# Signed search keys, a shorter tie step, halved first picks and a retuned order in a post-LN attention and routed-FFN kernel

## The reference

```python
qkv = x @ w_attn + b_attn
q, k, v = jnp.split(qkv, 3, axis=-1)
attn = softmax(q @ k.T / sqrt(C) + causal_mask)
x = _layernorm(x + (attn @ v) @ w_proj + b_proj)

scores = jnp.einsum('bld,d->bl', x, w_router)
_, top_idx = jax.lax.top_k(scores, k)            # k = int(0.75 * 4096)
out = x.at[batch_idx, top_idx].set(gelu(selected @ w_block))
x = _layernorm(x + out)
```

## Time and profile before

| | |
|---|---|
| three runs | 966.97, 969.17, 973.5 us |
| median | 969.17 us |
| the profiled execution's own time | 968.08 us |
| its span, from first to last instruction | 966.4 us |
| around the span | 1.68 us |
| mean granted TensorE clock | 0.989 |
| busy: PE, DVE, ACT, POOL | 939.0, 769.3, 635.3, 273.4 us |
| DMA | 149.53 MB, mean 155 GB/s |

### The profile page before, as it was taken

One profiled execution on the slowest core, in us unless ns is written; L12 is line 12 of the kernel. 1 busy time (PEld: TensorE's weight loads), 2 busy tenths in 40 slices (PEclk: granted clock), 3 DMA queues, 4 the chain that ended last, 5 costly groups with the idle time before them and its releaser, 6 DMA issues.

```text
span 966.4 us, 15640 instructions
## 1 busy us (share of the span) xinstructions
PE 939.0 (97%) x5078; PEld 805.6 (83%) x5078; DVE 769.3 (80%) x1473; ACT 635.3 (66%) x993; POOL 273.4 (28%) x436
## 2 busy tenths in 40 slices
PE   9999999999999999999999999999999999998991
PEld 7889988888888888888888999888888888887770
DVE  5688996967966786689769999887898778569977
ACT  3566675764864585478555875686688558447985
POOL 3523124253052034512214243323204302211162
PEclk9999999999999999999999999999999999999996
DMA  6535343344253345567433533535778534437935
GB/s 191 175 122 167 115 143 120 120 131 139 80 164 99 102 150 163 157 224 223 155 113 93 194 114 105 164 97 179 243 234 243 178 103 130 120 100 232 314 119 174
DMA packets 89378, 149.53 MB, mean 155 GB/s; under 512 B 7761, under 2 KB 25810, under 8 KB 89298
## 3 DMA queue, kind: packets, MB, share of 16 engines
q1 hardware_dynamic: 89298, 148.54, 48.9%
HBM read 108.66 MB, written 39.85 MB: 154 GB/s over the span
## 4 chain that ended last, share of the span: by engine, by line
PE 94%; DVE 3%; issue 1%; ACT 1%; POOL 0%; ACTq 0%; DVEq 0%; POOLq 0%
PE sbank L515 37%; PE fbank L515 13%; PE obank L1049 11%; PE obank L1051 11%; PE obank L1050 11%; PE obank L1043 2%; PE obank L1045 2%; PE obank L1044 2%; PE fbank L1340 1%; PE fbank L1139 1%; PE mbank L947 1%; PE mbank L970 1%; DVE cmp L1503 1%; PE obank L555 1%; ACT parts L996 0%
## 5 line engine op out<-in xcount | busy, mean ns | idle before, releaser
L515 PE MATMUL sbank<-qT,xT 128*128 128x512 f32 (+2 forms) x1728 | 413.2, 379 | 0.0
L515 PEld LDWEIGHTS sbank<-qT,xT 128*128 128x128 f32 x1728 | 306.4, 189 | 53.0 <-issue 0.3
L872 ACT COPY ring<-sbank 128x512 f32<-128x512 f32 (+3 forms) x288 | 157.6, 549 | 178.2 <-PE sbank L515 126.9
L1001 DVE TENSOR_TENSOR ring_lo<-ring,parts 128x1024 fp32r<-128x1024 f32 (+4 forms) x176 | 179.6, 1027 | 30.9 <-ACT parts L996 30.2
L1049 PE MATMUL obank<-ring_lo,vs 128*128 128x512 f32 x480 | 183.6, 383 | 4.3 <-ACT parts L996 2.6
L1051 PE MATMUL obank<-parts,vs 128*128 128x512 f32 x480 | 181.9, 379 | 0.0
L1050 PE MATMUL obank<-parts,vs 128*128 128x512 f32 x480 | 181.6, 378 | 0.0
L996 ACT CAST parts<-ring 128x1024 fp32r<-128x1024 f32 (+4 forms) x176 | 145.9, 834 | 51.7 <-PE obank L1051 38.9
L982 DVE TENSOR_TENSOR ring<-ring,mbank 128x1024 f32<-128x1024 f32 (+4 forms) x176 | 159.4, 946 | 9.4 <-PE mbank L970 9.4
L989 ACT ACTIVATE ring<-ring 128x1024 f32<-128x1024 f32 (+4 forms) x176 | 143.9, 844 | 24.7 <-DVE ring L982 24.4
L914 DVE TENSOR_TENSOR runmax<-ring,runmax 128x1024 f32<-128x1024 f32 x84 | 107.2, 1276 | 64.7 <-ACT ring L872 64.1
(11 more groups left out here) (222 smaller groups left out, 1203.6 us busy)
## 6 DMA issues: line engine op xcount, KB each, us to landing
vs<-v_scratch SPq DMA_DIRECT2D x288, 256.0 KB, 2.8
v_scratch<-vnew SPq DMA_DIRECT2D x30, 512.0 KB, 3.2
xres<-x SPq DMA_DIRECT2D x16, 512.0 KB, 4.6
out<-tail SPq DMA_DIRECT2D x32, 256.0 KB, 3.2
x_scratch<-xres SPq DMA_DIRECT2D x14, 512.0 KB, 3.0
y_scratch<-yb SPq DMA_DIRECT2D x14, 512.0 KB, 4.6
tail<-x_scratch SPq DMA_DIRECT2D x28, 256.0 KB, 3.5
tail<-y_scratch SPq DMA_DIRECT2D x28, 256.0 KB, 4.3
```

The costliest lines, as they stand in the source:

```text
L515: mm = eng.matmul(o, lhs(lh, k), rhs(rh, k), start=n == 0, stop=n == len(todo) - 1)
L872: act.copy(slot(n)[:, c0:], sbank[n % NSS][:, c0:]).then_inc(a_copy, 1)
L1001: dve.tensor_tensor(slots_lo(ns, c0), slots(ns, c0), f32(hi_of(u)), ALU.subtract).then_inc(v_lo, 1)
```

## The change

1. The planner's tables. `project xhi` goes from 4 to 15 and loses its margin of 2, `project vhi` and `softmax exp` lose their entries (100 and -4), `search first` goes from 60 to -4, `final pick` from 30 to -15, `ffn gelu` from 4 to 8. No other entry changes.
2. Keys. `make_keys` has three linked operations instead of four: the key stays a signed integer, its upper half is cut out with a mask instead of a shift and a multiplication, and the search of the upper half begins at -32768 * UPPER.
3. Ties. `split_ties` gets two operations more, which make one number per row out of the two marks; `select` has three linked operations instead of four.
4. The late block in the last search. `late_turn` lets each `stats` and the `aggr` of groups 14 and 15 wait for a certain comparison, for `split_ties` or for `select`; `pe_f` of the last group waits for `p_last`, a count that PE's rounds raise.
5. The first unit is picked and stored by single tiles (128 rows, 128 KB): 17 picks and 17 stores instead of 16.

```diff
-PREFER_US = {"ffn flo": 100, "final load": 100, "project vhi": 100, "ffn store": 100, "last chain": 60,
+PREFER_US = {"ffn flo": 100, "final load": 100, "ffn store": 100, "last chain": 60, "last router": 60,
...
-MARGIN_US = {"attention_out router": 3, "final scale": 3, "project xhi": 2, "ffn flo": 2, "final_roots": 2,
+MARGIN_US = {"attention_out router": 3, "final scale": 3, "ffn flo": 2, "final_roots": 2, "prepare bias": 1.5,
...
             def pe_f(pe, j, tiles_=(0, 1)):
+                if G == len(groups) - 1:
+
+                    pe.wait_ge(p_last, 2 + 2 * j + tiles_[0])
...
+            def late_turn(dve, t):
+
+                n = (G - LATE) * (QT + 1) + t
+                if n < 2 * ROUNDS - 1:
+                    dve.wait_ge(v_cmp, 2 * ROUNDS + 2 * (n + 2))
+                elif n == 2 * ROUNDS - 1:
+                    dve.wait_ge(v_sel, 2 * B)
+                else:
+                    dve.wait_ge(v_tie, B)
...
-                link(dve, dve.tensor_scalar(signs, bits, 31, -2147483648, ALU.arith_shift_right, ALU.bitwise_or))
+                signs = (mbank[:, 128:128 + NT].bitcast(I32) if b else top_keys[b])[:, k]
+                link(dve, dve.tensor_scalar(signs, bits, 31, 2147483647, ALU.arith_shift_right, ALU.bitwise_and))
                 link(dve, dve.tensor_tensor(keyi[:, 1, k], bits, signs, ALU.bitwise_xor))
-                link(dve, dve.tensor_scalar(keyi[:, 0, k].bitcast(U32), keyi[:, 1, k].bitcast(U32), 16, None,
-                                            ALU.logical_shift_right))
-                link(dve, dve.tensor_scalar(top_keys[b][:, k], keyi[:, 0, k], UPPER, None, ALU.mult))
+                link(dve, dve.tensor_scalar(top_keys[b][:, k], keyi[:, 1, k], -65536, None, ALU.bitwise_and))
...
+                dve.wait_ge(v_sel, 2 * (b + 1))
+                link(dve, dve.scalar_tensor_tensor(out=keyf[:, 2], in0=gteq[:, 0], scalar=2 * UPPER / (UPPER + TOPK),
+                                                   in1=gteq[:, 1], op0=ALU.mult, op1=ALU.add))
+                link(dve, dve.tensor_scalar(keyf[:, 2], keyf[:, 2], UPPER + TOPK, -UPPER, ALU.mult, ALU.add))
...
-                link(dve, dve.tensor_tensor_scan(ahead, ones[:, 0:2 * NT], tot, 0.0, ALU.mult, ALU.add))
-                dve.tensor_tensor(keyf[:, 2], ahead[:, NT - 1:2 * NT - 1], within, ALU.add).then_inc(v_tie, 1)
+                link(dve, dve.tensor_tensor(keyf[:, 2], keyf[:, 2], within, ALU.subtract))
+                dve.tensor_tensor_scan(ahead, ones[:, 0:2 * NT], tot, 0.0, ALU.mult, ALU.add).then_inc(v_tie, 1)
                 dve.wait_ge(v_tie, b + 1)
-                link(dve, dve.scalar_tensor_tensor(out=keyf[:, 0], in0=keyf[:, 2], scalar=float(TOPK), in1=gteq[:, 1],
-                                                   op0=ALU.is_lt, op1=ALU.mult))
-                link(dve, dve.scalar_tensor_tensor(out=left_out if b else sel[:, 1], in0=keyf[:, 0], scalar=0.0,
-                                                   in1=gteq[:, 0], op0=ALU.add, op1=ALU.is_equal))
+                link(dve, dve.tensor_tensor(left_out if b else sel[:, 1], ahead[:, NT - 1:2 * NT - 1], keyf[:, 2],
+                                            ALU.is_ge))
...
-            at("dve", "final pick", pick)
-            final_store(b, u, y, v_pick, u + 1)
+            if u:
+                at("dve", "final pick", lambda dve: pick(dve, 0, 2))
+                final_store(b, u, y, v_pick, u + 2)
+            else:
+
+                for t in range(2):
+                    at("dve", "final pick", lambda dve, t=t: pick(dve, t, t + 1))
+                    at("sp", "final store", lambda sp, t=t: store_half(sp, t))
```

More of the change, by code:

```diff
@@ L66 @@
-MARGIN_US = {"attention_out router": 3, "final scale": 3, "project xhi": 2, "ffn flo": 2, "final_roots": 2,
-             "prepare bias": 1.5, "out": 1.5, "ffn store": 1.5, "scores hide": 1, "values load": 0.6,
-             "ffn aggr": 0.6, "row_max reduce": 0.6, "values": 0.6, "project load": 0.3, "proj": 0.3,
-             "attention_out stats": 0.3}
+PREFER_US = {"ffn flo": 100, "final load": 100, "ffn store": 100, "last chain": 60, "last router": 60,
+             "project qhi": 60, "attention_out residual": 60, "project qlo": 60, "attention_out stats": 60,
+             "ffn fhi": 60, "attention_out score": 60, "row_max": 60, "final store": 60, "scores copy": 30,
+             "softmax hi": 30, "final pick": -15, "search": 30, "ffn stats": 15, "values load": 15,
+             "project xhi": 15, "prepare xlo": 8, "attention_out norm": 8, "ffn gelu": 8, "row_max reduce": 4,
+             "project vlo": 4, "softmax lo": 4, "project load": 4, "attention_out evac": 4, "prepare bias": 4,
+             "search first": -4, "scores hide": -4, "softmax z": -4, "final result": -4, "ffn add": -4,
+             "ffn aggr": -8, "attention_out router": -8, "attention_out aggr": -8, "attention_out istd": -8,
+             "last": -8, "final scale": -15, "final own": -15, "final choose": -30, "prepare": -30}
@@ L71 @@
+MARGIN_US = {"attention_out router": 3, "final scale": 3, "ffn flo": 2, "final_roots": 2, "prepare bias": 1.5,
+             "out": 1.5, "ffn store": 1.5, "scores hide": 1, "values load": 0.6, "ffn aggr": 0.6,
+             "row_max reduce": 0.6, "values": 0.6, "project load": 0.3, "proj": 0.3, "attention_out stats": 0.3}
 COSTS = {"pe": (.0, 1 / 2400, .2), "act": (.13, 1 / 1200, .14), "dve": (.09, 1 / 960, .12),
@@ L1404, in add @@
                 pool.tensor_tensor(y_pair(G, j), x1_pair(G, j), y_pair(G, j), ALU.add).then_inc(g_y, 1)
+            def late_turn(dve, t):
[6 more added lines that the diff above has]
+                    dve.wait_ge(v_tie, B)
             def stats(dve, t):
                 dve.wait_ge(g_y, 2 * G + t // 2 + 1)
+                if late:
+                    late_turn(dve, t)
                 if G and t == 0:
@@ L1412, in aggr @@
             def aggr(dve):
+                if late:
+                    late_turn(dve, QT)
                 for t in range(QT):
@@ L1438, in ffn @@
                 at("sp", "ffn store", store)
[L1441 removed]
+        SEARCH_STEPS = [3 + 2 + 2 * ROUNDS + 5, 2 * 3 + 2 + 2 * ROUNDS + 4]
         PIECES = [[(0, NT)], [(0, NT // 2), (NT // 2, NT)]]
@@ L1746, in both_outcomes, with pick @@
                 at("act", "final sums", lambda act, t=t: sums(act, t))
-            def pick(dve):
+            def pick(dve, t0, t1):
                 dve.wait_ge(v_srch, sum(SEARCH_STEPS[:b + 1]))
@@ L1815, in _ @@
             for n in range(2):
-                sp.wait_ge(st_o[n], 16 * B * NUT // 2)
+                sp.wait_ge(st_o[n], 16 * (B * NUT // 2 + (n == 0)))
         @block.gpsimd
```

14 lines of the change are left out of this document (8 added, 6 removed).

## The result

The changed kernel took 974.27 us in the median of 18 runs, the kernel before 969.14 in 18 runs beside it: a ratio of 1.005 with a 95% interval from 1.0038 to 1.0062. It is 5 us slower; the forecast was 970.5 and its range ended at 973.5. The sign was right and the size was not. The profiled execution of the changed kernel took 973.43 us, its span is 971.7 us against 966.4, so 5.3 us are to be found in the two traces. One run of all that follow, of the kernel fill_gap, took 1584.04 us where its nine others took 971 to 977, counts as slow and is left out of its ratio.

A forecast was written before the change was run, and what follows sets the result against it. PE, busy 939.0 of 966.4 us, was taken as the bound. Start +1.4, body 0 and tail -0.1 summed to +1.3, a span of 967.7, forecast as a 970.5 us median with range 967.0 to 973.5.

The forecast's parts named there:

- The pair on ACT: Start: the cast of the next group's x precedes the first queries' second half on ACT, making DVE's `qlo` 3.7 us late.
- The values begin at 21.9 instead of 20.47: +1.4 us: Start: PE waits for WV before the first values, a loss of 1.4 us; bounds +0.5 to +2.9.
- PE's own 20.9: Start, low bound: with no DVE operation slowed, the scores' end at 20.9 decides when values begin, +0.5 us.
- my bound of +2.9: Start, upper bound: both WB operations slowed and the scores' idle delaying the clock, +2.9 us.
- the tail's -0.1: Tail in all, from earlier mask and first store less store-queue gaps: about -0.1 us, bounds -0.9 to +0.5.
- The body (nothing): Body between start and tail: order swaps are covered by slack, 0 us, bounds -0.4 to +1.5; a failed cover costs 0.8 to 1.6.
- my rival of the early body: Early body: swapped casts of x wait for a load ahead of ACT's score copies, stopping PE; 972.2 us, chance 0.12.
- The search and the ties: Tail: last reduction 0.55 us earlier with the late product out of round 2's count; tie step gains 0.15.
- Picks and stores: Tail end: two statistics cost 0.66 before the first pick; half store leaves 0.32 earlier, store gaps take back about 0.28.
- The clock: Rival: pauses at the start make PE's clock rise 2.6 us later, costing 1.3 us; 971.8 us, chance 0.13.
- Not slower: Rival: x lands early or WV's slack covers the start, and the tail's gain comes through; 968.5 us, chance 0.2.
- the change doesn't do what it says: Rival: search rounds 3 and 4 lengthen by what round 2 gains, and statistics delay the picks; 971.0 us, chance 0.1.

The follow-up runs named there:

- fill_gap: Changed kernel with nine empty matmuls in PE's pause ahead of the first scores: 973.41 us, ratio 1.004 to the kernel before.
- swap_in: Kernel before with one swap on ACT: cast of the next group's x ahead of the second half of the first queries; 973.24 us, ratio 1.003.
- swap_back: Changed kernel with one swap on ACT: second half of the first queries again ahead of the cast of the next group's x; 971.1 us, ratio 1.0008.
- before_again: Kernel before, unchanged, profiled a second time: span 965.1 us.
- code_only: Changed kernel with the old planner tables, so only keys, ties, late block and halved first pick are new: 973.43 us, ratio 1.0026.
- xhi_back: Changed kernel with only the `project xhi` table entry as before (preference 4, margin 2): 969.15 us, ratio 0.999.
- after_again: Changed kernel, unchanged, profiled a second time: span 972.0 us.
- tables_only: Kernel before with the new planner tables (PREFER_US and MARGIN_US) alone: 974.4 us, ratio 1.0037.
- xres_later: Changed kernel with SP's two residual loads held back until the x of groups 1 and 2 has landed: 973.81 us, ratio 1.0027.
- best: Changed kernel, three moves: second queries before x's cast; copy near 406 before the activation; statistics and aggregation behind the fifth unit's pick. 969.08 us, ratio 1.0002.
- best_whole: Kernel best with the first unit picked and stored whole: 969.14 us, ratio 1.0002.
- best_hold: Kernel best with POOL's two subtractions for group 1 held back until both parts of WV are made: 968.59 us, ratio 1.0004.

## Why the prediction was right and wrong

**The pair on ACT.** Right, as worked out: ACT in order behind the cast, DVE in order behind `qlo`, WB's subtraction slowed to 1.65 to 1.67, its cast not (0.42), WV alone. By the Trainium skill's rule of the shared interfaces ("GPSIMD Engine Reference", section "8. Key points"), with the loser blocked ("SBUF — State Buffer", section "Terms"), I had named 22.2 for the case that both of WB's operations are blocked; the traces show the subtraction slowed and the cast not, and so the earlier value. WV's cast in the earlier trace rows had been slowed (1.55); why WB's was not stays open. I had WV ready at 21.7 to 22.2; in the five other profiles with this pair the values begin at 21.56 to 22.35. swap_in and swap_back show that the pair is the cause.

**The size of that term.** This is the step that failed: "The values begin at 21.9 instead of 20.47: +1.4 us". The first transposes of mcol, behind the start, show its whole price. Over five profiles with the old pair (before, before_again, swap_back, code_only, xhi_back) they stand at 36.11, 33.77, 36.02, 36.44 and 33.74, mean 35.2; with the new pair (after, after_again, swap_in, tables_only, xres_later) at 39.75, 39.01, 38.89, 39.57 and 39.10, mean 39.3. So the term is 4.1 us. That agrees with the 4.1 between the changed kernel and swap_back; swap_in put it at 2.9 (1.3 to 4.6). best, best_whole and best_hold have the old pair too and stand at 34.74, 37.86 and 35.00; with them the term is 3.8.

The 2.6 that I missed (4.05 less 1.43) have three parts, each rounded.

- 0.9: the base. 20.47 was the value of one execution, whose scores ran at half clock; over the five profiles the values begin between 18.10 and 20.80, mean 19.6.
- 0.4: the new value, 22.3 in the mean for 21.9.
- 1.4: what lies behind the first values, where my sum stopped. From there to the transposes it is 15.6 us in all five profiles with the old pair, and 17.2 to 17.4 in four of the five with the new one, since PE's waits for queries and WV were followed by half clock while it made the values (4.63 to 4.79 us for 24 products instead of 3.04).

In the old order PE is bound by its own clock at the start, and before_again and xhi_back, where it stayed up, gained 2.3; in best_whole it stayed up through the scores too, but WV came late. In the new order tables_only and xres_later had the scores at full clock and gained nothing by it: PE waited 1.80 for WV. With a low stretch on both sides the term is 3.1 (39.3 against 36.2), with none on either side 3.9 (fill_gap's 37.67 against 33.8): in neither case 1.4. The told that the clock was low in this stretch, and I carried it into both sides of the sum as if it were a property of the kernel. I had taken the low end of this term from "PE's own 20.9", where the low end of the old side was the number to ask for, and my bound of +2.9 was too low. The range had a second fault: its upper end adds the tail's -0.1 and not the tail's own bound of +0.5.

**The landing.** I had the cast at 14.68 as before. Over fourteen profiles it starts between 14.55 and 16.74, with the load issued between 8.3 and 8.9. In the old order that mostly costs nothing (best_whole's 2.20 is the exception); in the new one PE's scores start later by what the load is late, as after's 3.55 shows against 1.43 in after_again. At the transposes of mcol 0.7 of these 2.1 were left.

**The body.** I had written "The body (nothing)", with the wait of 0.8 to 1.6 as the price of a failed cover. It was +1.4 here, +0.8 of it at the wait near 409 (0.51 and the slower matmuls around it), and this one is no accident: it stands in all six profiles with the new entry for `project xhi` and no repair (0.51, 0.58, 1.17, 1.09, 0.56, 0.22) and at this place in none of the others. It is also the sign of being wrong that I had named, a new wait above 0.5. It is my rival of the early body with its place wrong: the mechanism is a copy of scores behind something that waits, but for POOL's roots, not for a load (the 1.10 in best_whole is the one for a load). I had compared the order around the old waits and not around the places where ACT waits for POOL. For the other 0.6, some of it near 700, I have no cause; the waits there come and go between profiles of one kernel.

**The search and the ties.** Right in kind: round 2 of the search lost its intruder. From the first reduction (935.06, now 940.17: 5.11 later) to the last (4.69 later) it gained 0.42, against 0.55 forecast; the tie step gained 0.15, as forecast.

**Picks and stores.** The two statistics cost 0.66 as forecast. The half store was issued 0.46 behind its pick (957.08 against 956.62) instead of 0.76, 0.30 earlier (0.32 forecast), and the stream of stores grew by 0.5, from 12.5 to 13.0, where I had 0.28. The first reduction had already come 0.25 late against PE (5.11 against 4.86), behind the late products at the head of the tail. So the tail came out 0.5 worse than forecast: +0.4 instead of -0.1. The sums weren't late: no pick waited for them.

**The rivals.** The clock, 0.13, came nearest: it was low longer, 6.8 us in after, after_again and swap_in. But tables_only and xres_later had the loss with half of that, and fill_gap had 3.9 of it against before_again with none at the start. So the clock is a part of the loss, the 1.4 behind the first values, and not its core. "Not slower" fell, as did "the change doesn't do what it says". No version that ran beats the kernel before by more than its interval.

## What to carry to other kernels

A profile is one execution. Before a difference to a number of it is formed, ask what in that number is the kernel's and what the execution's: a stretch at low clock, a load that landed early. The second profile of the same kernel, with its 18.14, moves my main term from 1.4 to 3.8; the two together would have shown how little one of them says.

A term also doesn't end where the first late instruction starts: hold the two traces side by side some way behind it. On an engine that runs in order, putting a step that waits for a DMA ahead of one that waits for nothing costs as soon as anything hangs on the second, whatever the planner's estimate of the landing says; here the margin of 2 on the stream that waits kept the old order. And a preference that looks like a loss (picks behind statistics, 0.66) may be what keeps a wait of 3 us off the end; take it away in an experiment before calling it one.

## What was not expected of the hardware

The clock. In 6 of the 13 profiles that follow the first it fell to half near 886 to 893 for some 3.4 us, behind PE's waits of 1.65 and 1.41 there, and cost some 1.5 us (42.3 us from the second wait to the first transposes of the tail, 40.8 in the others); in the others, with the same two waits, it didn't. In swap_back it fell for 3.4 us at 934.6. At the start it was low for 3.4 us in four of the eight profiles with the old pair. In best_whole it fell behind the wait of 2.20 for WV. In before, swap_back and code_only PE had no wait just ahead, but one of 0.72 to 0.73 us for DVE's A near 9 us; in the four profiles where the clock stayed up this wait was 0.23 to 0.48. No run varies that wait, so it may be a coincidence.

POOL's small operations. One of 128x4 takes 0.20 us, and took 1.05 to 1.18 where it met a DVE operation of 1.22 (L914, L1001) that reads two tensors in SBUF. The page "SBUF — State Buffer" of the Trainium skill, section "Terms", says that the loser is blocked for the whole instruction. The trace agrees: 1.18 less 0.20 is 0.98, and of DVE's operation, which began 0.10 earlier, 1.12 were left.

The load of x. 512 KB that were issued at 8.3 to 8.9 us landed after 6 to 8 us. Holding back 1 MB behind them changed nothing that could be seen (14.88). What sets the landing stays open.
